# Loading a position band in two rounds around a weight load, in the opening of a fused attention and feed-forward kernel

## What is computed

```python
idx = jnp.clip(rel + MAX_REL, 0, NUM_BUCKETS - 1)
bias = jnp.transpose(rel_table[idx], (2, 0, 1))
scores = jnp.einsum('bhtd,bhsd->bhts', q, k) * scale + bias[None]
scores = jnp.where(causal[None, None], scores, jnp.float32(-jnp.inf))
w = jax.nn.softmax(scores, axis=-1)
...
x = x + _layernorm(_L0_attn_ref(_layernorm(x, axis=-1), ...), axis=-1)
x = x + _layernorm(_L0_ffn_ref(_layernorm(x, axis=-1), ...), axis=-1)
```

## Time and profile before

| | us |
|---|---|
| median of three runs | 2115.11 |
| lowest, highest | 2114.58, 2115.66 |
| profiled execution, its own time | 2117.22 |
| span of the profiled execution | 2115.4 |
| TensorE matmul busy | 2054.7 (97%) |
| VectorE busy | 1883.9 (89%) |
| ScalarE busy | 1768.0 (84%) |
| GpSimd busy | 1800.9 (85%) |

### The profile page before, as it was taken

How to read it: one execution, slowest core, us unless ns; L and a number is a source line. 1 busy time by engine, 2 the same in 40 slices (tenths; PEclk the granted TensorE clock), 3 DMA queues, 4 the chain that set the end, 5 groups by cost and what they waited for, 6 DMA issues and landing times.

```text
span 2115.4 us, 76117 instructions
## 1 busy us (share of the span) xinstructions
PE 2054.7 (97%) x29965; PEld 1388.0 (66%) x29965; DVE 1883.9 (89%) x4973; ACT 1768.0 (84%) x2671; POOL 1800.9 (85%) x1492
## 2 busy tenths in 40 slices
PE   4999999999999999999999999999999999999997
PEld 2566666666666666666666666666666666666676
DVE  6898889999999999999999999999999998888867
ACT  4889988888888888888888888888888888888865
POOL 3678888988988988988988988988988988888883
PEclk9999999999999999999999999999999999999999
DMA  7111122313223322223322323323223322222271
GB/s 185 42 52 52 52 65 72 82 50 74 65 67 74 82 52 72 65 65 77 82 50 74 65 65 77 79 50 77 65 65 77 77 52 66 58 58 69 62 148 37
DMA packets 337924, 147.98 MB, mean 70 GB/s; under 512 B 173344, under 2 KB 336800, under 8 KB 337568
## 3 DMA queue, kind: packets, MB, share of 16 engines
q1 hardware_dynamic: 337568, 143.12, 28.4%
HBM read 25.04 MB, written 43.06 MB: 32 GB/s over the span
## 4 chain that ended last, share of the span: by engine, by line
PE 53%; DVE 28%; issue 10%; POOL 3%; ACT 2%; DMA 2%; SPq 1%; DVEq 1%; POOLq 0%; ACTq 0%
PE score_ps L826 10%; DVE row_max L1971 7%; PE misc L779 7%; PE misc L916 6%; PE misc L918 5%; PE misc L917 5%; PE max_ps L873 5%; PE score_ps L832 3%; DVE v_calc L1944 3%; DVE tail L2022 3%; DVE score_ps L1989 3%; PE misc L797 2%; PE misc L949 2%; POOL probs L2768 2%; PE misc L954 2%
## 5 line engine op out<-in xcount | busy, mean ns | idle before, releaser
L2768 POOL TENSOR_TENSOR probs<-probs_f,probs 128x1024 f16<-128x1024 f32 (+3 forms) x704 | 1119.4, 1601 | 198.4 <-ACT probs L1443 193.5
L1423 ACT ACTIVATE probs_f<-score_ps,score_unit 128x1024 f32<-128x1024 f32 (+3 forms) x704 | 620.5, 881 | 240.0 <-DVE score_ps L1989 111.1
L1971 DVE TENSOR_REDUCE row_max<-max_ps 128x2 f32<-128x1024 f32 (+1 forms) x634 | 624.6, 1002 | 5.5 <-PE max_ps L882 5.3
L1443 ACT CAST probs<-probs_f 128x1024 f16<-128x1024 f32 (+3 forms) x704 | 574.2, 816 | 17.8
L916 PE MATMUL misc<-v_pair,probs 128*128 128x65 f16 x4608 | 439.3, 193 | 0.8 <-DVE o_norm L2001 0.5
L917 PE MATMUL misc<-v_pair,probs 128*128 128x64 f16 x4608 | 438.2, 193 | 0.0
L918 PE MATMUL misc<-v_pair,probs 128*128 128x65 f16 x4608 | 437.4, 193 | 0.0
L916 PEld LDWEIGHTS misc<-v_pair,probs 128*128 128x128 f16 x4608 | 416.7, 97 | 26.6 <-issue 19.4
L917 PEld LDWEIGHTS misc<-v_pair,probs 128*128 128x128 f16 x4608 | 417.7, 97 | 0.7
L918 PEld LDWEIGHTS misc<-v_pair,probs 128*128 128x128 f16 x4608 | 417.9, 97 | 0.0
L779 PE MATMUL misc<-xT,w_split 128*128 128x512 f16 x1512 | 361.1, 381 | 0.9 <-DVE v_calc L1944 0.9
(11 more groups left out here) (291 smaller groups left out, 3731.3 us busy)
## 6 DMA issues: line engine op xcount, KB each, us to landing
v_pair<-v_calc SPq DMA_DIRECT2D x64, 516.0 KB, 3.9
o_scratch<-o_stage SPq DMA_DIRECT2D x128, 256.0 KB, 3.3
xh<-x SPq DMA_DIRECT2D x56, 128.0 KB, 3.0
x_res<-x SPq DMA_DIRECT2D x56, 128.0 KB, 3.0
out<-tail SPq DMA_DIRECT2D x56, 128.0 KB, 1.7
shift_all<-shift_row SPq DMA_DIRECT2D x256, 1.0 KB
probs<-wqkv SPq DMA_DIRECT2D x3, 1024.0 KB, 7.7
probs<-band_scratch SPq DMA_DIRECT2D x8, 144.0 KB, 3.9
```

The lines of the kernel that those rows point to most:

```text
L1423: nc.scalar.activation(dst, score_ps[t % 2][:, :, 0:width], ACT.Exp, scale=score_unit[:]).then_inc(exp_done, 1)
L1443: nc.scalar.copy(dst, src).then_inc(hi_done, 1)
L1971: last = dve.tensor_reduce(dst[:, :, i % 4:i % 4 + 1], tile[:, :, col:col + width], AX.X, ALU.max)
L2768: pool.tensor_tensor(low, copy_of(par + ahead, t)[:, 0:2 * width], high, ALU.subtract).then_inc(lo_done_pool, 1)
```

## The change

The band is loaded in two rounds. `load_bands` gets a range of pairs. The first round, 8 DMAs for the first pair alone (32 partitions x 144 elements, 18 KB each), is issued before the third part of the weights; the second round, 8 DMAs for the other seven pairs (126 KB each), behind it. Ahead of the second round SP waits until the first has landed, so that the counts of the semaphore band_in stay unambiguous. ScalarE waits for 8 landings (a count of 128) before it scales the first pair, and for all 16 (a count of 256) before it scales the rest.

```diff
-            def load_bands():
+            def load_bands(start, end):
                 held(band_out, 32)
+                held(band_in, 16 * 8 if start else 0)
                 for first in range(0, P, REPEAT):
                     r, within = first // D, first % D
                     for h in range(2):
-                        sp.dma_start(band[D * h + within:D * h + within + REPEAT, :, r, :],
-                                     shifted(0, first)[:, h::2, 0:WIN]).then_inc(band_in, 16)
+                        sp.dma_start(band[D * h + within:D * h + within + REPEAT, start:end, r, :],
+                                     shifted(0, first)[:, 2 * start + h:2 * end:2, 0:WIN]).then_inc(band_in, 16)
...
                 load_head(NB)
                 store_bands()
+                load_bands(0, 1)
                 load_weights(2)
-                load_bands()
+                load_bands(1, NPAIR)
                 load_bandT()
...
             def scale_band(pairs):
                 act.wait_ge(vec_setup, QK_READY)
-                act.wait_ge(band_in, 16 * 8)
+                act.wait_ge(band_in, 16 * 16 if pairs.start else 16 * 8)
```

## The result

| | before | changed |
|---|---|---|
| median, us | 2115.88 | 2121.38 |
| lowest, highest | 2114.22, 2116.56 | 2119.51, 2123.11 |
| runs | 11 | 11 |
| profiled execution: its time, its span | 2117.22, 2115.4 | 2120.46, 2118.7 |

The ratio is 1.0026, with a 95% interval of 1.0019 to 1.0034: slower by 5.5 us, where +5.3 had been forecast. Measured again in a later batch the ratio was 1.0023 [1.0014, 1.0033], 4.6 us.

What follows compares the result with a forecast made beforehand. Dense TensorE work fills 97% of the span; its start hangs on bandT's landing. bandT +5.5, stores 0, clock 0 and second count 0 sum to 5.5, rounded down to +5.3: median 2120.4 us, range 2117.7 to 2122.8.

Steps and rivals of the forecast that it cites:

- The first round, 3.9 us: SP's 8 small band loads for the first pair take 3.9 us to issue, bounds 2.7 and 6.0.
- The stores, 0: The band's stores, with no weights behind them, land no sooner: 0 us, bounds -1.0 and 0.
- The third part of the weights, landing at 31.6: Issued at 25.9 instead of 7.14, this load takes 5.7 us and lands at 31.6 instead of 25.3, no longer hidden.
- The second wait, 1.0: SP waits for the first round's landing until 27.4 instead of going on at 26.4, delaying the second round and bandT.
- bandT 5.5 late: bandT lands at 42.5 instead of 37.0, worked out by issues (42.4) and by bytes (42.6); bounds +3.3 and +7.6.
- ScalarE: Scales the first pair's band at about 27.5 instead of 30.63, but the 3 us gained end in its wait for bandT.
- VectorE and TensorE: After the weights, q1 and k1 start at 35.3, take up to 4.9 us; k1 ready at 40.2, 2.3 ahead of bandT.
- The clock, 0: TensorE's clock at the first fills brings no gain: 0 taken, 1.1 us of gain as the bound.
- A (the rate): Band loads run as fast as issued, at 422 GB/s; k1 then decides, +2.7 us; chance 0.07.
- C (the weights as the path): Weights sharing the queue land after 33.9, so k1 comes last: +6.1 or +8.1 us; chance 0.13.
- B: bandT is late by less than 4.2 us, +3.3 or so, through cheap issues, early stores or clock; chance 0.18.
- D: Faster, through earlier stores, faster band loads and full-clock q1 and k1 together; chance 0.04, including unseen later gains.

Runs made afterwards that it cites:

- the moved line: Kernel before, with ScalarE scaling bandT's first two heads after q0 of the second pair instead of ahead of k1's high part: 2109.51 us, ratio 0.9973.
- the repeat pair: Both kernels, unchanged, measured and profiled once more: before 2114.33 us, ratio 0.9996; changed 2119.34 us, ratio 1.0023.
- bandT was out of the way: Changed kernel, with ScalarE's scaling of bandT moved behind q0 of the second pair: 2117.83 us, ratio 1.0014.
- none of 3 with it: GpSimd's o_stage subtraction in step 2 waits for VectorE's 6x6 multiplication: changed kernel 2119.53 us, before 2114.86, before with bandT's scaling also moved 2110.40.

## Why the prediction was right, step by step

- **What bounds the opening.** Right: bandT ahead of k1 on ScalarE. It is shown by the wait in the changed kernel, by what the moved line gained on the kernel before, and by the first fill, which moved with the time in every variant.
- **The first round, 3.9 us.** 3.56 us from 20.80, 0.46 each at most.
- **The stores, 0.** They landed at 20.74, 1.2 sooner than in the earlier trace rows. But a second profile of before has 20.80 with the weights behind them, so the change has no part in it; the 0 was right, and the profile that it was taken from was late.
- **The third part of the weights, landing at 31.6.** Issued at 24.41, 5.4 us to land, 29.8. The 5.7 was good. The 1.8 us are the stores (1.2), cheaper issues (0.3) and the landing (0.3). find_top starts 4.4 us later than in the earlier trace rows, 4.6 and 5.6 in the other two pairs: the load is uncovered, as the step says.
- **The second wait, 1.0.** SP was free at 24.84 and went on at 25.77: 0.93. But the step that let the whole 1.0 run through to bandT failed: without the wait bandT was only 0.25 us sooner, since the weights kept the engines busy.
- **bandT 5.5 late.** 4.5 in the mean of three pairs of profiles, 3.1 in the pair that the forecast was about. Its last load took 8.59 us and not 9.26. The two workings do not differ by their numbers: from the measured landing of the weights the one by bytes gives 29.8 + 11.7 - 0.7 = 40.8, from the measured last issue the one by issues 31.48 + 9.26 = 40.7, and it landed at 40.07. That an issue 1.06 us sooner moved bandT by only 0.25 speaks for bytes. Neither named the reason: from 20 to 26 us the small loads leave the engines three quarters idle, and the band and bandT behind, at 201 to 234 GB/s, do not make up for it.
- **ScalarE.** Right: the 3 us gained ended in the waits for q1 and bandT. But the wait for bandT, which was to be 5 us or more and the longest one of all loads, was 3.35, and VectorE's for the weights was 7.26. The prediction's own numbers gave less than 5: with q1 and k1 at half the clock from 35.3, q1's high part would have ended at about 38.4, and bandT was to land at 42.5.
- **VectorE and TensorE.** 3.66 us from find_top to q1, as taken. The 12 matmuls took 5.30 us, above the 4.9 given as the most: the 2.46 for six that it doubles came from a stretch in which the granted clock was rising (0.50 from 41 to 42 us, 0.80 from 42 to 43), and six at 0.50 throughout took 2.74. k1 was ready at 38.75, 1.3 ahead of bandT and not 2.3; in the second profile, where the 12 took 4.28, it was 2.5.
- **The clock, 0.** Right in this profile: the granted clock was 1.00 up to 42 us, so the first fills ran at the full clock, but it was 0.67 from 42 to 43 and 0.50 behind, and q0 took 2.74 us. The bound of 1.1 was a little small: with k1 repeated that row was 1.27 shorter.
- **The sum.** +5.3 forecast, +5.5 and +4.6 measured. Some of the agreement is luck: bandT's term was 1.0 too large by the mean of the profiles, and what the medians have beyond the first fill, 1.0 us in the first measurement and 0.1 in the second, is not explained. "The end moves by the amount of the first fill" holds to 1 us: for the repeat pair the first fill is 5.3 us later and the profiled time (2113.28, 2118.11) 4.8 longer, for the first pair 3.1 and 3.2, with the luck told above. The claim that I am wrong if the first fill starts before 41 was cut close at 41.31.
- **The rivals.** A (the rate) fell: 201 to 234 GB/s, as in the earlier trace rows. The Trainium skill, page "DMA: Bandwidth & Descriptors", section "Specifications", would have had these loads at the full line rate; the stretches disagree, with 576-byte rows at about half of the weights' 406 GB/s and the engines' share at 1.17 to 1.22. Which of the rows' length, their uneven place in DRAM or the 32 partitions of each load makes them slow, no run here separates. C (the weights as the path) did not come about in this kernel, but it was near: once bandT was out of the way, it alone put the first fill 6.85 us later. B did not happen by the medians, but the profiles come close to it: bandT was 4.5 us late in the mean, where B ends at 4.2, and 3.1 in the first pair. D did not happen.

## What to carry to other kernels

A load that is needed early and one that only fills a gap are not exchanged for free: the gap is then left to small transfers that cannot fill it, and the loads behind are late by most of the time that the DMA engines stood empty. Before reordering loads to release an engine's first wait, look at its next one. Here, moving one operation behind a few compute steps took the late load off the path and gained 0.27%, where every order of the loads that was tried lost. And take at least two profiles of the kernel before you work out a difference of a few us from one.

## What was not expected of the hardware

- **A tiny VectorE operation held by GpSimd.** 6x6 elements take 0.22 us, or 1.28 us when GpSimd's o_stage operation starts some 0.1 us behind. It was long in 7 of 11 profiles without the wait and in none of 3 with it. GpSimd's start lay 102 to 104 ns behind VectorE's in the seven long ones and 108 to 116 in the seven short ones, so the two groups lie 4 ns apart, and the same program falls on either side. The Trainium skill, page "SBUF — State Buffer", section "Who interferes with whom", has some instructions of VectorE, `tensor_scalar` in its two-port modes among them, contend with GpSimd for a shared pair of ports: whichever issues first holds it for its whole instruction and the other waits. That the long one ends with GpSimd's operation agrees with such a wait. It is VectorE's record that starts first, though, and VectorE that is held, so the order in which the two took the ports can't be read from these rows.
- **Small loads.** 18 KB land 1.75 us after their issue and 1 MB of weights after 5.4. The issue of a band load takes about the same whatever it carries (0.42 us for 18 KB, 0.45 for 126 and 144, with a gap of 0.04 behind), so 8 small loads hold the queue at 37 to 42 GB/s.
- **The same transfer, differently long.** In two profiles of the kernel before bandT's last load took 9.26 and 7.61 us, in both of the changed kernel 8.59. The transposition at 60 us took 3.94 to 4.37 us in these four, and 5.34 where k1 was repeated, with nothing changed about it. That is up to a third of what is measured here.
